# A decoder kernel: the selective-scan stage in units of one width, with two sets of accumulators

## The reference

```python
gate = jax.nn.sigmoid(x @ W_gate.T + b_gate)
proj = x @ W_in.T + b_in
x_proj, delta_proj = jnp.split(proj, 2, axis=-1)          # 512 channels each
delta = jax.nn.relu(delta_proj)
A = -jnp.exp(A_log)                                        # 512 x 16 states
h = h * jnp.exp(A * d_t[..., None]) + (x_t * d_t)[..., None] * B_mat
y_t = h @ C_mat[0]                                         # one step of the scan over t
return gate * (y + x_proj * D_vec) @ W_out.T + b_out
```

## Time and profile before

| | before |
|---|---|
| median of 3 runs | 3762.36 us (3757.89 to 3763.67) |
| the profiled execution | 3764.46 us |
| its span, first to last instruction | 3762.7 us |
| TensorE busy over the span | 3167.4 us (84%) |
| VectorE busy | 1726.6 us (46%) |
| ScalarE busy | 1224.6 us (33%) |
| GpSimd busy | 303.9 us (8%) |
| mean granted TensorE clock | 0.894 |
| all 192 scans (L3222) | 289.5 us of VectorE |

### The profile page before, as it was taken

One profiled execution on the slowest core, in us unless ns is written; L12 is line 12 of the kernel. 1 busy time (PEld: TensorE's weight loads), 2 busy tenths in 40 slices (PEclk: granted clock), 3 DMA queues, 4 the chain that ended last, 5 costly groups with the idle time before them and its releaser, 6 DMA issues. The chain is left out here.

```text
span 3762.7 us, 57675 instructions
## 1 busy us (share of the span) xinstructions
PE 3167.4 (84%) x23550; PEld 2016.1 (54%) x23550; DVE 1726.6 (46%) x3003; ACT 1224.6 (33%) x2523; POOL 303.9 (8%) x520
## 2 busy tenths in 40 slices
PE   6997699999989977699999979798874787788594
PEld 3664465566578866456555656565552232245473
DVE  4664344444423224444444432255366788736112
ACT  1332244444511122144444421232232755513010
POOL 1020000000000000000000000001011000101101
PEclk9998799999989987699999989899685889868697
DMA  2001000000100020000000000000100000000332
GB/s 99 12 16 57 10 2 2 2 2 1 54 14 0 0 71 24 10 2 1 2 2 2 23 21 13 31 21 9 23 34 14 1 1 1 1 18 12 133 119 78
DMA packets 41715, 88.24 MB, mean 23 GB/s; under 512 B 7867, under 2 KB 35340, under 8 KB 37900
## 3 DMA queue, kind: packets, MB, share of 16 engines
q1 hardware_dynamic: 37132, 78.09, 6.1%
q0 software_dynamic: 1536, 4.20, 0.4%
q10 hardware_dynamic: 2816, 2.62, 0.2%
HBM read 55.50 MB, written 9.44 MB: 17 GB/s over the span
## 5 line engine op out<-in xcount | busy, mean ns | idle before, releaser
L2213 ACT ACTIVATE prob<-R,neg_max 128x333 f32<-128x333 f32 x512 | 271.6, 536 | 326.7 <-DVE neg_max L2279 325.9
L3222 DVE TENSOR_TENSOR_SCAN arena<-arena 128x512 f32<-128x512 f32 (+1 forms) x192 | 289.5, 1562 | 49.4 <-PE R L3055 31.9
L2279 DVE TENSOR_REDUCE neg_max<-R 128x2 f32<-128x666 f32 x256 | 216.7, 847 | 54.0 <-PE R L2111 39.8
L2285 DVE COPY prob_t<-T 128x384 f32<-128x384 f32 x256 | 141.9, 554 | 195.9 <-PE T L2122 184.9
L2122 PEld LDWEIGHTS T<-const,prob 128*128 128x128 f32 (+1 forms) x1536 | 183.3, 143 | 65.5 <-issue 40.2
L2122 PE MATMUL T<-const,prob 128*128 128x128 f32 (+1 forms) x1536 | 210.2, 273 | 2.5 <-DVE prob_t L2285 2.0
L2071 PE MATMUL O<-arena,keys_in 128*128 128x512 f32 (+1 forms) x384 | 186.9, 612 | 13.5 <-ACT arena L2192 6.9
L3155 ACT ACTIVATE arena<-delta,neg_a 128x510 f32<-128x510 f32 (+1 forms) x192 | 162.2, 859 | 97.6 <-DVE arena L3222 95.8
L3055 PE MATMUL R<-arena,diag 64*64 64x512 f32 x1024 | 146.1, 685 | 44.8 <-DVE arena L3222 44.8
L2066 PE MATMUL O<-keys_in,arena 128*128 128x333 f32 x512 | 177.2, 473 | 6.7 <-DMA keys_in<-ctx_nt 5.5
L2296 DVE TENSOR_TENSOR attn_t<-O,arena 128x256 f32<-128x256 f32 x128 | 54.4, 425 | 274.3 <-ACT arena L2225 274.3
(11 more groups left out here) (465 smaller groups left out, 5662.9 us busy)
## 6 DMA issues: line engine op xcount, KB each, us to landing
w<-w_dram SPq DMA_DIRECT2D x16, 1024.0 KB, 7.5
arena<-pack_dram SPq DMA_DIRECT2D x2, 4608.0 KB, 16.0
q_pad<-q_pad SPq DMA_DIRECT2D x24, 224.0 KB, 2.7
arena<-pack_dram SPq DMA_DIRECT2D x4, 1284.0 KB, 6.4
arena<-pack_dram SPq DMA_DIRECT2D x1, 4873.0 KB, 14.6
arena<-k_nat SPq DMA_DIRECT2D x16, 224.0 KB, 2.8
arena<-arena SPq DMA_DIRECT2D x16, 224.0 KB, 2.8
arena<-pack_dram SPq DMA_DIRECT2D x1, 2707.0 KB, 15.1
```

The source lines that it names most:

```text
L2213: last = nc.scalar.activation(prob[:, g % 2, i, :], S.R[:, g % 2, i * BANK:i * BANK + XK], ACT.Exp, bias=neg_max[:, g % 2, i:i + 1], accum ...
L2279: nc.vector.tensor_reduce(neg_max[:, g % 2, :], S.R[:, g % 2, :].rearrange("p (i n) -> p i n", i=2)[:, :, 0:XK], AX.X, ALU.max, negate=Tru ...
L2285: nc.vector.tensor_copy(prob_t[:, m % 2, 0, :, qt * P:(qt + 1) * P], S.T[:, 0, 0:3 * P].rearrange("p (c q) -> p c q", c=3)).then_inc(M.pt_ ...
L3222: nc.vector.tensor_tensor_scan(state[:, q % HELD, 0:width(i)], decay[:, q % DEEP, 0:width(i)], u[:, i % 2, 0:width(i)], 0.0, ALU.mult, ALU ...
```

## The change

All units are two batches wide (512 columns), so there are 16 of them and 256 steps. `S.R` is used as two sets of accumulators, one for even and one for odd units, so `skipped(i)` waits for `product(i-2)` in place of `product(i-1)`, and the swap of a unit moves from its end to the next unit, behind the sum of steps 2 and 3. `odd_part` moves from after decay 3 to after decay 6, `product` from after scan 3 to after scan 6, `weighted` from after scan 11 to after scan 8, `inputs` and `gates` on ScalarE by one step each. The output product of a batch is summed in PSUM as units end: four matmuls per unit, behind the sum of steps 8 and 9 of the next unit; the bias goes in first. Residuals and norms of both batches of a group stand after scans 11, 13 and 15 of the next group's first unit; their transposes stand on TensorE after the sum of steps 14 and 15 of that unit, ahead of the drain, and after the first sum of the next. Held decays go from 3 to 6 and held states from 6 to 10; both are now 512 columns each. The gate is computed as tanh: sigmoid(z) = (1 + tanh(z/2)) / 2, where the halves go into B·C, D and the gate's bias, and the product becomes (tanh + 1)·sum in one instruction.

```diff
+    CT, NS, DEEP, HELD, PAIR = 4, 16, 6, 10, 2
+    UNITS = B // PAIR * CT
+    STEPS = UNITS * NS
...
-        decay = W[:, used:used + DEEP * WIDE].rearrange("p (s n) -> p s n", s=DEEP)
-        u = W[:, used + DEEP * WIDE:used + (DEEP + 2) * WIDE].rearrange("p (s n) -> p s n", s=2)
-        top = W_COLS - HELD * WIDE
+        decay = W[:, used:used + DEEP * BANK].rearrange("p (s n) -> p s n", s=DEEP)
+        top = W_COLS - HELD * BANK
         state = spare[:, top:W_COLS].rearrange("p (s n) -> p s n", s=HELD)
-        xp = sb("xp", [P, 2, WIDE])
...
+
+        def sums(i, a):
+            return S.R[:, i % 2, a * BANK:(a + 1) * BANK]
 
         block = ctx.enter_context(nc.Block())
...
+            def deltas(i):
+                if i >= 1:
+                    pe.wait_ge(M.g_done, i)
+                project(i, "wd", S_d, M.qa_full)
+
+            def gates(i):
+                pe.wait_ge(M.d_done, i + 1)
+                project(i, "wg", S_d, M.qa_full)
+
+            def inputs(i):
+                if i >= 1:
+                    pe.wait_ge(M.x_done, i)
+                project(i, "wx", S_x, M.qd_full)
 
             def skipped(i):
-                g, ct = UNITS[i]
-                if i >= 1:
-                    pe.wait_ge(M.prod_done, i)
+                if i >= 2:
+                    pe.wait_ge(M.prod_done, i - 1)
                 pe.wait_ge(M.x_done, i + 1)
...
+                for a in range(2):
+                    for h in range(2):
+                        rows, to = slice(h * HB, (h + 1) * HB), (h + a) % 2 * HB
+                        last = nc.tensor.matmul(sums(i, a)[to:to + HB, :], diag[rows, i % CT, n + a, :], state[rows, (q + a) % HELD, :],
+                                                start=(a == 1 and n == 0), stop=False, skip_group_check=True)
                 last.then_inc(M.state_used, 2)
...
                 pe.wait_ge(M.odd_sb, i + 1)
+                nc.tensor.matmul(sums(i, 0), swap[:], odd[:], start=False, stop=True, skip_group_check=True).then_inc(M.pv_full, 1)
+
+            def output(i):
+                g, ct = i // CT, i % CT
+                if ct == 0:
+                    if g >= 1:
+                        pe.wait_ge(M.xt_done, PAIR * g)
+                    for s in range(PAIR):
+                        for tt in range(TT):
+                            nc.tensor.matmul(S.O[:, s, tt * D:(tt + 1) * D], part(S.const, CONST, "ones")[0:1, :],
+                                             part(W, TB, "bo")[0:1, :], start=(tt == 0), stop=False, skip_group_check=True)
+                pe.wait_ge(M.prod_done, i + 1)
+                for s in range(PAIR):
+                    for tt in range(TT):
+                        at = s * T + tt * P
+                        last = nc.tensor.matmul(S.O[:, s, tt * D:(tt + 1) * D], gated[:, i % 3, at:at + P], wout[:, ct, :],
+                                                start=False, stop=(ct == CT - 1), skip_group_check=True)
+                    if ct == CT - 1:
+                        last.then_inc(M.y_full, 1)
 
...
-            for i in range(len(UNITS)):
+            for i in range(UNITS):
+                g, ct = i // CT, i % CT
                 skipped(i)
                 for n in range(0, NS, 2):
                     summed(i, n)
-                    q = i * NS + n + 1
-                    if i + 1 < len(UNITS) and n in (0, 2, 6):
-                        project(i + 1, {0: "d", 2: "x", 6: "g"}[n])
-                    if q in outputs:
-                        output(outputs[q])
-                    if q in turns:
-                        transposed(turns[q])
+                    if n == 0:
+                        if g >= 1 and ct == 1:
+                            transposed(PAIR * g - 1)
+                        if i + 1 < UNITS:
+                            deltas(i + 1)
+                    if n == 2:
+                        if i >= 1:
+                            swapped(i - 1)
+                        if i + 1 < UNITS:
+                            inputs(i + 1)
+                    if n == 6 and i + 1 < UNITS:
+                        gates(i + 1)
+                    if n == 8 and i >= 1:
+                        output(i - 1)
+                    if n == 14 and g >= 1 and ct == 0:
+                        transposed(PAIR * g - 2)
                 pe.drain().then_inc(M.odd_full, 1)
-                swapped(i)
-            output(B - 2)
-            output(B - 1)
+            swapped(UNITS - 1)
+            output(UNITS - 1)
             transposed(B - 2)
             transposed(B - 1)
...
             def gates(i):
-                g, ct = UNITS[i]
-                evacuated(i, "g", gated[:, g % 2, ct, 0:width(i)], ACT.Sigmoid)
-                act.drain().then_inc(M.g_done, 1)
+                act.wait_ge(M.qa_full, 2 * i + 2)
+                nc.scalar.activation(gated[:, i % 3, :], S_d, ACT.Tanh, bias=half_bg[:, i % CT, :], scale=0.5).then_inc(M.g_done, 1)
 
...
-            for i in range(len(UNITS)):
-                g, ct = UNITS[i]
+            for i in range(UNITS):
+                g, ct = i // CT, i % CT
                 for n in range(NS):
                     decays(i, n)
-                    q = i * NS + n
-                    if i == 0 and n == 3:
+                    if i == 0 and n == 4:
                         gates(0)
-                    if i >= 1 and n == 3:
-                        odd_part(i - 1)
-                    if i + 1 < len(UNITS):
+                    if i + 1 < CT:
+                        diagonal(i + 1, n)
+                    if n == 6:
+                        if i >= 1:
+                            odd_part(i - 1)
+                        if g >= 1 and ct == 1:
+                            transposed(PAIR * g - 2)
+                    if n == 8 and g >= 1 and ct == 1:
+                        transposed(PAIR * g - 1)
+                    if i + 1 < UNITS:
                         if n == 9:
                             deltas(i + 1)
-                        if n == 10:
+                        if n == 11:
                             inputs(i + 1)
-                        if n == 13:
+                        if n == 14:
                             gates(i + 1)
-                    if i + 1 < CT:
-                        diagonal(i + 1, n)
-                    if q in turns:
-                        transposed(turns[q])
-            odd_part(len(UNITS) - 1)
+            odd_part(UNITS - 1)
             transposed(B - 2)
...
             def weighted(i):
-                n = width(i)
-                dve.wait_ge(M.qb_done, 3 * i + 2)
-                nc.vector.tensor_tensor(u[:, i % 2, 0:n], xp[:, i % 2, 0:n], delta[:, i % 2, 0:n], ALU.mult)
+                dve.wait_ge(M.d_done, i + 1)
+                dve.wait_ge(M.x_done, i + 1)
...
             def product(i):
-                g, ct = UNITS[i]
-                n = width(i)
                 dve.wait_ge(M.pv_full, i + 1)
                 dve.wait_ge(M.g_done, i + 1)
-                nc.vector.tensor_tensor(gated[:, g % 2, ct, 0:n], gated[:, g % 2, ct, 0:n], S.R[:, 0, 0:n], ALU.mult)\
+                nc.vector.scalar_tensor_tensor(gated[:, i % 3, :], gated[:, i % 3, :], 1.0, sums(i, 0), ALU.add, ALU.mult)\
                     .then_inc(M.prod_done, 1)
 
...
             dve.wait_ge(S.weights_ready[k], 16)
-            b_at, c_at = SCAN["b"][0], SCAN["c0"][0]
-            nc.vector.tensor_tensor(bc[:], scan[:, :, b_at:b_at + NS], scan[:, :, c_at:c_at + NS], ALU.mult)
+            nc.vector.scalar_tensor_tensor(bc[:], all_of("b"), 0.5, all_of("c0"), ALU.mult, ALU.mult)
+            nc.vector.tensor_scalar(half_bg[:], all_of("bg"), 0.5, None, ALU.mult)
...
+            for i in range(UNITS):
+                g, ct = i // CT, i % CT
+                leaving = g >= 1 and ct == 0
                 for n in range(NS):
                     scanned(i, n)
-                    q = i * NS + n
-                    if n == 3 and i >= 1:
+                    if n == 6 and i >= 1:
                         product(i - 1)
-                    if n == 11 and i + 1 < len(UNITS):
+                    if n == 8 and i + 1 < UNITS:
                         weighted(i + 1)
-                    if q in outputs:
-                        residual(outputs[q])
-                    if q in norms:
-                        normalised(norms[q])
-            product(len(UNITS) - 1)
+                    if n == 11 and leaving:
+                        residual(PAIR * g - 2)
+                    if n == 13 and leaving:
+                        normalised(PAIR * g - 2)
+                        residual(PAIR * g - 1)
+                    if n == 15 and leaving:
+                        normalised(PAIR * g - 1)
+            product(UNITS - 1)
             for b in (B - 2, B - 1):
                 residual(b)
                 normalised(b)
```

(44 more changed lines are left out.)

128 lines of the change are left out of this document (39 added, 89 removed).

## The result

The changed kernel takes 3696.7 us (median of 4 runs, 3692.1 to 3699.8) against 3760.1 us beside it: ratio 0.983, 95% interval 0.981 to 0.985, 63 us less. The forecast was 3702.

What follows compares the result with a forecast made beforehand. VectorE was the longest chain, unsaturated, with waits at unit edges. Chain 322.4 plus waits 11.6 gives 334.0 us instead of 390.1; with the tail's −5.4, −61.5 from 3764.5 profiled, stated as 3702; range 3689 to 3726.

Steps and rivals of the forecast that it cites:

- VectorE's chain: VectorE's work in the scan stage: 256 scans, weightings, products and six batches' residuals and norms, together 322.4 us.
- plain unit: A unit without residuals or norms: 16 scans, a weighting and a product on VectorE, 19.1 us; TensorE 17.7 us.
- Waits: VectorE's remaining or new waits in the scan stage, 11.6 us in sum.
- the weighting in unit 0: weighted(1) waits for inputs queued behind twelve decays, the gate and the deltas on ScalarE: 1.6 us, new.
- the product in unit 1: A milder half-clock wait in unit 1, as unit 0 has no swap or output product: 1.0 us.
- the products after a leaving pair: After a finished group's two batches do residuals and norms, the next unit's late swap delays product: 2.5 us, three times.
- first residuals: First residual of a finished group's two batches waits for its output matmuls: 0.5 us, three times, 1.5 us.
- The clock: TensorE falls to half clock after idle time where batches leave, delaying the next swap: 7.5 us over three units.
- The tail: From last scan to next stage: first residual's wait falls 4.1 us, the second's 1.3 us, together −5.4 us.
- rival 2: TensorE follows too closely, half clock as units begin: 3731 us if in most units, 3716 in half; chance 0.27.
- rival 3: The gate's table loads stay, 32 of them, costing 5 to 12 us: 3707 to 3714 us; chance 0.05.
- Slower than before: TensorE stays at half clock through the stage, nearly 35 us a unit: 3940 us; chance 0.03.

Runs made afterwards that it cites:

- the second profile: The changed kernel itself, unedited, profiled again at the end beside the best version on one chip: ratio 0.9829 to the kernel before, 3694.0 us, stretch 334.7 us.
- the kernel with spare matmuls: Changed kernel plus spare 512-column TensorE matmuls in the three units where finished batches leave: ratio 0.985 to the kernel before, 3700.4 us.

## Why the prediction was right

The forecast of the stage was 61.5 us less and it is 61.0. By its own terms, in the first profile:

- *VectorE's chain*: 322.4 us forecast, and 334.4 less the waits below, 11.4, gives 323.0. The plain unit was put at 19.1 us and is 19.05. The new form of the product costs 0.58 to 0.61 us by starts, the same as the old (0.60).
- *Waits*: 11.6 us forecast. Measured: the weighting in unit 0 1.18 (1.6 forecast; the pitch with diagonals is 0.85, not 0.87), the product in unit 1 1.18 (1.0), the products after a leaving pair 1.84, 1.84 and 1.73 (2.5 each), first residuals 3 × 0.58 (0.5 each). Four products of 0.35 to 0.38 us in the units behind these were not forecast, nor was a gap of 0.43 us in one batch's statistics. Sum 11.4. That the sums agree within 0.2 us is luck: the leaving pairs were put 2.1 us too high, and 1.9 us that nobody forecast stand against it. In the second profile the parts are others again (2.03 in unit 2, 1.10, 1.47 and 1.49 after leaving pairs), with 11.7 in all.
- *The clock* as cause of the waits after leaving pairs is shown: kept at full there, they vanish. The size was 0.7 us too high each time, in part because the first sum of the next unit was nearly at full speed again (1.22 us; 0.5 more than 1.09 was forecast). The forecast has the clock fall only after idle time; the falls behind one-row matmuls with the engine busy, 2 us of wait each, it doesn't have, and the first profile happened to have none.
- *The tail*: −5.4 us forecast, 20.9 to 15.7 is −5.2. The first residual waits 1.22 us (1.2 forecast), the second not at all.
- *TensorE close behind at full clock, rival 2 refuted*: plain products don't wait, and 294.5 us of 334.4 are busy, 88%.
- *The gate*: no load was left, and rival 3's price is measured with the sigmoid kept, 3.7 us, a little under its 5 to 12. The Trainium skill ("ScalarE: Activation LUTs", Table sets), with exp and tanh in one set, agrees with the trace: no load between them in the stage.
- *Slower than before* needed TensorE at half clock for more than two fifths of its work; its mean clock is 0.94.

Where the prediction's reasons were thin: it gave held states and decays a role as reserves ("With ten states VectorE is stopped only when TensorE lags by about eight scans", "Six decays cover 6.7 us of interruption"). No run refutes the sentences, but neither names what the two numbers do. The states bring nothing in time at ten that they don't at six. The decays matter not as cover but because the wait for scan n − DEEP holds up everything queued behind that decay; at three, with the new places, the change would have lost 23.7 us of its gain.

How the gain divides can't be read as a sum. Of the stretch, width alone costs 27, tanh alone brings 21 in the old order and 4 in the new, taking the second set away costs 44, taking three decays away costs 24.

Open: why the sums' waits fell too with tanh alone; how much of the 44 us belongs to the second set and how much to places tuned for it; whether the last 2 to 3 us of the measured gain (63.4 in the medians, 61.0 in the stage) are more than scatter; and what decides whether the clock falls behind one-row matmuls.

## What to carry to other kernels

Two engines of nearly equal load lose at each handover that runs around a loop (drain, copy, swap, product, skip), so a second accumulator set can be worth narrower, dearer units; count its price first, here 27 us. When a ring of buffers is deepened or cut, look at what stands behind the instruction that waits for the ring: moving two copies out of PSUM one place forward each did nearly all that three more buffers did. An instruction placed at a fixed point of a busy engine's order should stand just behind the time when its input is there by the other engine's queue, half clock included; two places later took away 8 us of waits here.

## What the runs showed of the hardware

The granted clock of TensorE fell from full to about half right behind four matmuls with one-row weights though the engine was busy without a gap (0.57 from 3023 to 3027 us in the kernel with spare matmuls; 0.54 from 2936 to 2938 in the second profile of the changed kernel). Such a fall stands in 10 of 40 places with one-row matmuls, 8 times with no idle time ahead of it and twice (three decays held) behind some 1 us of it. In one place the same program had it in one execution and not in another, so the one-row matmuls don't bring it down alone. With the same bias from 128-row weights it stayed at 1.00 in 4 of 4 places, and the output matmuls behind took 1.89 us in place of 3.38 to 3.68.

GpSimd's two small instructions for rstd (128x2) take 1.04 and 1.46 us beside running scans of 512 columns; in the kernel before, beside scans of 1024, they took 2.10 and 2.53 us. The Trainium skill ("GPSIMD Engine Reference", the table of TRN2 properties) says that the SBUF interfaces are shared with VectorE and contended by its instructions with two SBUF inputs; a scan has two, and the trace agrees: in the tail, with no scan running, those of the kernel before took 0.22 and 0.71 us:

```profile
3304.73 0.22 POOL L3295 TENSOR_SCALAR rstd<-mv 128x2 f32<-128x2 f32 x1 [72.44 <-DVE mv L3242]
3305.10 0.71 POOL L3297 TENSOR_TENSOR rstd<-rstd,const 128x2 f32<-128x2 f32 x1
```
